# Stage 1 of a Mamba and expert layer: who copies the last column of each scanned state

## The reference

```
delta = softplus(dt_low @ dt_proj_w.T + dt_proj_b)
dA    = exp(delta[..., None] * A)
dBu   = delta[..., None] * B_var[:, :, None, :] * ut[..., None]
h     = da * h + dbu                      # for every time step, from h = 0
y     = einsum('bdn,bn->bd', h, c)
```

## Time and profile before

| | |
|---|---|
| median of the runs shown | 4303.94 us |
| profiled execution, device time | 4303.73 us |
| its span, first to last instruction | 4302.0 us |
| what lies around the span | 1.73 us |
| busy over the span: DVE, POOL, ACT, PE | 87%, 83%, 81%, 82% |
| copies `hlast<-h` on ACT | 511, 103.0 us by their records |
| products `dbu` on POOL | 511, 2431.5 us by their records |

### The profile page before, as it was taken

The page is one execution under the profiler, slowest core; times in us unless marked ns, Lnnn a source line. Parts: engine busy times, 40 slices in busy tenths (PEclk is TensorE's granted clock), DMA queues, the critical chain, the costliest instruction groups (busy, mean ns, idle before and its releaser), DMA issues. The chain is left out here.

```text
span 4302.0 us, 57736 instructions
## 1 busy us (share of the span) xinstructions
PE 3515.3 (82%) x19574; PEld 2483.7 (58%) x19574; DVE 3740.1 (87%) x4796; ACT 3477.8 (81%) x5917; POOL 3565.7 (83%) x1883
## 2 busy tenths in 40 slices
PE   7778888888888887888888888888876399999993
PEld 3455555555555555555555555555555289989882
DVE  5899999999999999999999999999997666665665
ACT  5899999989999999999999999999885066565663
POOL 3899999999999999999999999999886256666667
PEclk9999999999999999999999999999987599999996
DMA  2667777677676676776776777666665223333346
GB/s 85 153 159 168 170 173 168 163 176 172 157 167 167 157 167 163 172 172 167 170 174 164 168 168 175 163 167 167 152 152 119 51 64 64 72 69 65 64 128 251
DMA packets 178855, 628.41 MB, mean 146 GB/s; under 512 B 33648, under 2 KB 97264, under 8 KB 119168
## 3 DMA queue, kind: packets, MB, share of 16 engines
q0 software_dynamic: 73920, 368.61, 42.5%
q1 hardware_dynamic: 104640, 256.10, 17.8%
HBM read 223.57 MB, written 68.68 MB: 68 GB/s over the span
## 5 line engine op out<-in xcount | busy, mean ns | idle before, releaser
L463 POOL TENSOR_TENSOR dbu<-du,bb 128x2048 f32<-128x2048 f32 x511 | 2431.5, 4810 | 103.0 <-DVE h L939 78.0
L939 DVE TENSOR_TENSOR_SCAN h<-da,hlast,dbu 128x512 f32<-128x512 f32 x1536 | 1867.5, 1265 | 78.0 <-POOL dbu L463 52.8
L791 PE MATMUL ht<-ident,h 128*128 128x128 f32 x8192 | 1175.7, 288 | 456.1 <-DVE h L939 177.4
L524 ACT ACTIVATE da<-dl,negA 128x512 f32<-128x512 f32 x2048 | 1413.7, 702 | 117.2 <-DVE h L939 112.0
L791 PEld LDWEIGHTS ht<-ident,h 128*128 128x128 f32 x8192 | 965.0, 147 | 870.2 <-DVE h L939 320.6
L543 ACT ACTIVATE pair<-ht,ct 128x512 f32<-128x512 f32 x896 | 592.3, 689 | 123.3 <-PE ht L791 66.1
L939 DVE TENSOR_TENSOR_SCAN h<-da,dbu 128x512 f32<-128x512 f32 x512 | 592.6, 1206 | 45.0 <-POOL dbu L463 23.8
L715 PE MATMUL spare<-xin,win 128*128 128x512 f32 x1024 | 495.1, 613 | 11.9 <-DMA xin<-in_xt 7.4
L724 PE MATMUL spare<-xh,conv 128*128 128x512 f32 x1024 | 466.1, 598 | 0.8 <-ACT xh L555 0.8
L1705 ACT ACTIVATE hraw<-f,b 128x512 f32<-128x512 f32 x256 | 176.5, 690 | 221.3 <-PE f L1789 192.8
L447 POOL DMA_DIRECT2D acc<-pair x222 | 227.0, 1023 | 144.1 <-ACT pair L543 60.2
(11 more groups left out here) (244 smaller groups left out, 5719.0 us busy)
## 6 DMA issues: line engine op xcount, KB each, us to landing
acc<-pair POOLq DMA_DIRECT2D x222, 1024.0 KB, 7.2
bb<-b_rows SPq DMA_DIRECT2D x128, 1024.0 KB, 6.3
acc<-acc POOLq DMA_DIRECT2D x64, 1024.0 KB, 7.9
dl<-du POOLq DMA_DIRECT2D x62, 512.0 KB, 5.8
x_scores<-scores_and_rows SPq DMA_DIRECT2D x33, 512.0 KB, 4.5
xin<-in_xt SPq DMA_DIRECT2D x32, 512.0 KB, 4.9
sums<-scores_and_rows SPq DMA_DIRECT2D x32, 512.0 KB, 6.3
scores_and_rows<-in_x SPq DMA_DIRECT2D x31, 512.0 KB, 4.0
```

Source lines behind the costliest of these rows:

```text
L463: pool.tensor_tensor(dbu[n % 2][:], du[q][:], bb[part % 2][:, m:m + 1, :].to_broadcast([P, DT, CH]), ALU.mult).then_inc(dbu_done, 1)
L524: act.activation(da[DA_SLOT[m]][:], dl[q][:, dt, :], ACT.Exp, scale=negA[:, dt, n:n + 1]).then_inc(exp_done, 1)
L791: last = te.transpose(ht[HT_SLOT[m]][:, dt * P:(dt + 1) * P], h[n % 2][:, dt, b * P:(b + 1) * P], ident[:])
L939: dve.tensor_tensor_scan(h[n % 2][:, dt, :], da[DA_SLOT[n * DT + dt]][:], dbu[n % 2][:, dt, :], start, ALU.mult, ALU.add).then_inc(scan_do ...
```

## The change

The copy of a state's last column moves from ScalarE to GpSimd. `save_last` for the state two back in the program (it crosses from chunk to chunk) is issued at the head of each state's work on GpSimd, ahead of that state's product. Its wait on `scan_done` has the same value as the wait that the product has anyway, since the product overwrites the `dbu` tile that the state two back has used. The last two states of the program are not saved, so there are 510 copies in place of 511.

```
@@ gpsimd @@
+                def save_last(c, n):
+
+                    pool.wait_ge(scan_done, (c * NS + n + 1) * DT)
+                    pool.tensor_copy(hlast[:, n, :], h[n % 2][:, :, CH - 1]).then_inc(last_saved, 1)
+
...
                 def chunk(c, pos, groups, ahead, scan=True):
                     q = pos % 2
                     for n in range(NS):
+                        if not (is_first(c) and n < 2):
+                            save_last(*divmod(c * NS + n - 2, NS))
                         if scan:
@@ scalar @@
-                def save_last(c, n):
-
-                    act.wait_ge(scan_done, (c * NS + n + 1) * DT)
-                    act.copy(hlast[:, n, :], h[n % 2][:, :, CH - 1]).then_inc(last_saved, 1)
-
...
-                            if k == 2 and n == 0 and before:
-                                save_last(c - 1, NS - 1)
-                            if k == 2 and n > 0 and scan:
-                                save_last(c, n - 1)
```

## The result

The changed kernel takes 4327.98 us (median, 4326.87 to 4331.76) against 4304.31 us of the kernel before. The ratio is 1.0056, with a 95% interval of 1.0043 to 1.0068: slower by about 24 us. Forecast were 4321 us, slower by 17. The profiled execution's span grew from 4302.0 to 4325.1 us.

A forecast was written before the change was run, and what follows sets the result against it. DVE was taken to set the pace, waiting most for POOL's products. Places A 0.48, B 0.10 and C 0 gave 0.58 us per chunk, times 30 chunks 17.4 us, on 4303.7: 4321.1 us, range 4302 to 4348.

The forecast's parts named there:

- price x: Time one added copy costs POOL, bounded by neighbouring instructions between 0.08 and 0.32 us and taken as 0.14.
- upper end of 0.32: Highest price of a copy on POOL: a tiny step recorded with its whole duration and a gap; total then 4366 us.
- Place A: States 15 to 3: five copies ahead of just-in-time products delay the scans, up to 0.48 us per chunk at state 3.
- tie of POOL to DVE: State 15's product starts right behind state 13's last scan; from there to state 5's product POOL shows no wait.
- Place B: States 6 to 9: 0.18 us won on ACT against 0.28 us of added copies, so 0.10 us lost per chunk.
- the copies ahead of 6 and 7 vanish in half a microsecond: POOL has about half a microsecond before the sum's DMA at 1008.89, which covers the copies ahead of products 6 and 7.
- Place C: States 10 to 13: POOL's 1.13 us DMA wait covers copies 10 and 11, and 12's adds nothing; 0 us.
- room of state 2: In states 15 to 3, time between state 2's product and its scan that absorbs copy delay; counted as 0.22 us.
- price of 0.16 us: Alternative price of a POOL copy, from the Trainium skill's dispatch figures; said to make the sum about 5 us larger.
- Hidden copies: Rival: POOL copies are dispatched during the product ahead and cost 0.05 us or less; 4303 to 4307 us, chance 0.20.
- ScalarE as what held DVE: Rival: relieving ACT shrinks DVE's waits for `da`, state 6 above all, making the kernel faster; 4295 us, chance 0.07.
- The dear copy: Rival: behind state 15 a waiting POOL copy finishes before its product starts, 0.3 us five times; 4335 to 4366, chance 0.13.

The follow-up runs named there:

- e6: The kernel before, with one of GpSimd's four du products moved from behind state 15's product to behind state 14's; 4304.14 us, ratio 1.0010.
- e7: The changed kernel, with one du product on GpSimd moved from behind state 15's product to behind state 14's; 4325.70 us, ratio 1.0056.
- e4: The changed kernel with only the copies of states 3, 4 and 5 on GpSimd, the other thirteen back on ScalarE; 4304.38 us, ratio 1.0007.
- e2: The changed kernel without any copies or DVE's wait for them, the scans starting from columns of zeros; 4295.83 us, ratio 0.9988.
- e3: The changed kernel with the five copies ahead of the products of states 15, 0, 1, 2 and 3 back on ScalarE; 4314.75 us, ratio 1.0027.
- e10: Like e3, with the copies of states 9 to 12 also back on ScalarE; GpSimd keeps seven, ahead of products 4 to 10; 4305.63 us, ratio 1.0005.
- e5: The changed kernel with each copy made twice on GpSimd, once into a small tile that nobody reads; 4363.22 us, ratio 1.0150.
- e1: The changed kernel with ScalarE also making each copy, into a tile nobody reads, and VectorE waiting for both; 4330.73 us, ratio 1.0067.
- e9: The changed kernel with each GpSimd copy issued behind the product it stood ahead of; 4340.32 us, ratio 1.0085.

## Why the prediction was right

**Who bounds.** Right. Over the 28 chunks of the table DVE's recorded busy time grew by 0.15 us per chunk, out of 0.68, and its idle time in front of scans by 0.82, while its waits ahead of other work shrank. The waits for products grew by 24.3 us. I had written 90 to 110 us for those waits and 100.8 came. For `da` I had written about 35, from 40.6; it is 39.7. The 0.2 us that ScalarE wins at state 6 is real (state 7 falls from 0.20 to -0.01 in the table). Over 28 chunks that is 6 us, but the waits for `da` fell by only 0.9 in all, so other waits for `da` must have grown; which ones wasn't looked into.

**The price x.** 0.14 us was taken, 0.11 to 0.13 between ends and 0.15 between starts were measured. The nearest row, the halo copy, was the right one. The upper end of 0.32 had no basis in what followed.

**Place A, states 15 to 3.** 0.48 us were forecast. The trace gives 0.26 from state 15 to the next state 0 and 0.20 from there to state 3: 0.46. The size was right but not its parts. The step that named a tie of POOL to DVE ahead of state 15's product failed: e6, e7 and the starts of the products show that the run of POOL's work mostly begins before it. In the trace before, POOL is idle for 1.0 us per chunk ahead of the sum's DMA behind state 10 and for 1.3 ahead of the one behind state 11, and for 0.1 in all from there to state 15's product. The copy ahead of state 0's product is almost free: the product starts 0.08 us behind the end of the `du` row (1066.82 + 6.01 = 1072.83). Before the change it did so as well (1059.24 + 5.24 = 1064.48 against 1064.56 in the earlier trace rows), by this row:

```profile
1059.24 5.24 POOL L399 TENSOR_TENSOR du<-dl,u 128x512 f32<-128x512 f32 x4
```

So the copy, dispatched at 1071.74, fits into a gap that was there. On the mean state 15's product ends 0.65 us late in its chunk, and the next chunk starts 0.68 late. The copies ahead of 12 to 14 count in its place: the product of 11 ends 0.28 us late in its chunk, that of 14 0.54. This delay uses up the room of states 14 and 15 and comes out at the next state 0. That the two errors cancel is luck.

**Place B, states 6 to 9.** 0.10 us were forecast, 0.13 came (0.20 at state 3, 0.33 at state 9; standard error 0.08). Again the parts differ: about nothing was forecast for state 8 and 0.14 behind it for state 9, but 0.10 came at state 8 and 0.03 behind it. e4 shows ScalarE's 0.2 us won at state 7 and waited away at state 8 while copies stand ahead of the products of 5, 6 and 7. Without any copies (e2) most of it is kept. So the step by which the copies ahead of 6 and 7 vanish in half a microsecond was wrong in part: in the trace before, POOL is idle for only 0.13 us per chunk ahead of the sum's DMA behind state 7, and for 0.01 in the changed kernel.

**Place C, states 10 to 14.** Forecast as zero; it is 0.09 in the changed kernel, which the scatter of one trace can't tell from nothing (standard error 0.11), and 0.27 between states 11 and 14 once place A is cleared (e3). e10 shows by its time, 10 us nearer to the kernel before than e3, that the four copies there cost something. So this term was mis-sized, for the reason given under place A, and the changed kernel pays for most of it at the next state 0.

**The sum.** 0.68 us per chunk in place of 0.58, with a standard error of 0.14. 28 chunks make 19.0 of the 21.4 us by which stage 1 ends later; 1.0 comes before the first scan and 1.4 from the four chunks at the ends, of which I had counted two in full (1.2 us) and two at nothing. Another 1.7 us of the profiled difference of 23.1 lie behind stage 1. The change has no part in what stands before the first scan, and that scan starts anywhere from 2 us earlier to 1 us later than before in the traces of the experiments, so I take this part for scatter. Of the 6 us that the profiled run lies above the forecast, 3 are the 28 x 0.10 of the chunks, and the other 3 lie in the three parts just named. In the prediction itself the room of state 2 should read 0.25 us, not 0.22, and the price of 0.16 us adds 4 us, not 5; neither changes the sum.

**The rivals.** Hidden copies are refuted by e2 and e5. ScalarE as what held DVE is refuted by the result's direction, e1 and e4, though e2 grants it 7 us when nothing is put in its place. The dear copy is refuted by the starts and ends in the timeline. That each copy costs the same wherever it stands is refuted by e3 and e10, each time narrowly, and by e5, where the second set costs more than the first. The spread of DVE's idle time over the chunk was only argued for places that no run isolates, the copies ahead of 6 to 8 among them.

## What to carry to other kernels

Before moving a small instruction from one busy engine to another, find out for which of the two the bottleneck engine waits, and at which items; the same instruction costs its price where the product is just in time and little where there is room a few items further on. A start right behind its releaser isn't proof of an idle engine: compare it with the end of the work ahead, and do so over many periods, not one. An instruction whose result is needed late goes ahead of the long one that everybody waits for, not behind it.

## What the runs showed of the hardware

A copy of 128x4 recorded with a mean of 0.55 us on GpSimd takes 0.13 us of its time, and the same copy recorded with 0.20 us on ScalarE takes 0.09. The records of GpSimd's copies range from 0.18 to 1.51 us, so in a full queue they hold mostly waiting. And a scan that waits for a short GpSimd copy issued directly behind the product starts 0.33 us after the product (e9), in place of 0.03 to 0.04 where it waits for the product alone. The copy's own place in the queue is 0.13 of the 0.29 added: at the end of a chain a short instruction costs more than the time that it takes from its engine. What the other 0.16 us are no run shows.
